# A decoder layer on one core: places of the shared TensorE units by a table, one projection row a slot earlier, residual rows fetched a slot ahead

## The reference

```
x = x + self_attention(layernorm(x))        # causal, q and k normalised per head, softmax
x = x + cross_attention(layernorm(x), ctx)  # per query row only the 32 largest of 512 scores enter the softmax
x = x + ffn(layernorm(x))                   # inner 2048, rows quantised to 8 bits, weights to -1, 0, 1
ffn(x) = quant(silu(quant(x) Wg) * (quant(x) Wu)) Wd
```

## Time and profile before

| | |
|---|---|
| median of 3 runs | 3952.01 us (3951.01 to 3952.15) |
| the profiled execution | 3955.8 us |
| its span, first to last instruction | 3954.0 us |
| mean granted TensorE clock | 0.86 of full speed |
| DVE busy / PE busy / ACT / POOL | 3219.5 / 3320.5 / 2451.1 / 1916.0 us |
| mean of one MAX8 (L876) / MATCH_REPLACE8 (L881) | 680 / 676 ns |
| chain that ended last | DVE 38%, PE 28%, POOL 13%, issue 9% |

### The profile page before, as it was taken

One profiled execution on the slowest core, in us unless ns is written; L12 is line 12 of the kernel. 1 busy time (PEld: TensorE's weight loads), 2 busy tenths in 40 slices (PEclk: granted clock), 3 DMA queues, 4 the chain that ended last, 5 costly groups with the idle time before them and its releaser, 6 DMA issues.

```text
span 3954.0 us, 61337 instructions
## 1 busy us (share of the span) xinstructions
PE 3320.5 (84%) x18502; PEld 2447.8 (62%) x18502; DVE 3219.5 (81%) x7571; ACT 2451.1 (62%) x4921; POOL 1916.0 (48%) x2444
## 2 busy tenths in 40 slices
PE   2587788998989989998989898998999898877765
PEld 1355576766666667666766676766766676555542
DVE  4311199999989999899989898899979998999961
ACT  3343466666766667666866676667766676555533
POOL 0123234446655465546654555445654564355435
PEclk7667888988989989988988898988898898887778
DMA  8112332332222222322222222322232221211100
GB/s 277 50 51 57 98 77 69 81 86 66 71 66 77 66 62 77 97 76 62 78 78 78 70 67 63 84 72 68 78 82 79 73 70 41 62 46 35 33 22 19
DMA packets 167443, 283.04 MB, mean 72 GB/s; under 512 B 40639, under 2 KB 52939, under 8 KB 166606
## 3 DMA queue, kind: packets, MB, share of 16 engines
q1 hardware_dynamic: 160782, 275.98, 25.6%
q10 hardware_dynamic: 6336, 3.15, 0.3%
HBM read 113.27 MB, written 31.46 MB: 37 GB/s over the span
## 4 chain that ended last, share of the span: by engine, by line
DVE 38%; PE 28%; POOL 13%; issue 9%; ACT 5%; SPq 3%; DMA 1%; DVEq 0%; POOLq 0%; ACTq 0%
DVE cW L881 17%; DVE top L876 14%; PE bank L682 6%; PE bank L607 5%; PE bank L654 4%; POOL srs L1147 3%; SPq L513 3%; PE bank L593 2%; POOL hh L1111 2%; DVE smx L1013 2%; PE bank L670 2%; PE bank L635 2%; POOL hh L1115 2%; PE bank L694 2%; PE bank L701 2%
## 5 line engine op out<-in xcount | busy, mean ns | idle before, releaser
L881 DVE MATCH_REPLACE8 cW<-top,cW 128x512 f32<-128x512 f32 x1536 | 1026.3, 676 | 0.0
L876 DVE MAX8 top<-cW 128x8 f32<-128x512 f32 x1536 | 980.8, 680 | 0.0
L797 ACT ACTIVATE PT<-bank 128x512 f32<-128x512 f32 (+3 forms) x1024 | 539.6, 527 | 363.5 <-PE bank L593 359.8
L1168 POOL TENSOR_TENSOR cS<-cS,cW 128x512 f32<-128x512 f32 x512 | 641.7, 1275 | 199.3 <-ACT cW L825 198.8
L607 PE MATMUL bank<-cv,PT 128*128 128x33 f32 x4096 | 589.0, 291 | 113.3 <-ACT PT L797 111.8
L607 PEld LDWEIGHTS bank<-cv,PT 128*128 128x128 f32 x4096 | 559.1, 211 | 148.1 <-ACT PT L797 141.6
L607 PEld LDWEIGHTS bank<-sv,PT 128*128 128x128 f32 x2560 | 404.8, 214 | 81.1 <-ACT PT L797 57.4
L1175 POOL TENSOR_SCALAR cnb<-top 128x2 f32<-128x2 f32 x256 | 49.0, 191 | 807.4 <-DVE top L876 793.1
L593 PE MATMUL bank<-ident,cS 128*128 128x128 f32 x2048 | 352.2, 300 | 82.4 <-POOL cS L1168 82.4
L825 ACT ACTIVATE cW<-cW,cnb 128x512 f32<-128x512 f32 x512 | 347.6, 733 | 118.5 <-DVE cW L881 118.1
L607 PE MATMUL bank<-sv,PT 128*128 128x33 f32 x2560 | 377.0, 282 | 37.2 <-ACT PT L797 36.0
(11 more groups left out here) (151 smaller groups left out, 6105.0 us busy)
## 6 DMA issues: line engine op xcount, KB each, us to landing
sk_stack<-part SPq DMA_DIRECT2D x512, 64.0 KB, 2.0
sq_stack<-part SPq DMA_DIRECT2D x512, 64.0 KB, 2.0
ck_stack<-part SPq DMA_DIRECT2D x512, 64.0 KB, 2.0
cq_stack<-part SPq DMA_DIRECT2D x512, 64.0 KB, 2.0
w_group<-wa_by_group SPq DMA_DIRECT2D x32, 768.0 KB, 4.5
w_group<-wc_by_group SPq DMA_DIRECT2D x32, 768.0 KB, 4.3
feed<-in_x SPq DMA_DIRECT2D x32, 256.0 KB, 3.0
feed<-in_ctx SPq DMA_DIRECT2D x32, 256.0 KB, 3.0
```

Of the source, the lines that this page charges most:

```text
L797: act.activation(PT[k][:, 0:n], turned_ps[k][:, 0:n], ACT.Copy).then_inc(turned_read, step("turned_read", label))
L876: dve.max(top8[:, j, r, :], src[:]).then_inc(topk, step("topk", (c, r, "max", j)))
L881: dve.match_replace(cW[j][:], top8[:, j, r, :], src[:], REPLACED).then_inc(topk, step("topk", (c, r, "replace", j)))
L1168: pool.tensor_tensor(cS[m % 2][j][:], cS[m % 2][j][:], cW[j][:], ALU.subtract).then_inc(cprob, step("cprob", (m, j)))
```

## The change

It puts the tables of `schedule(b)` in the place of the formulas, for each batch element b:

- cross tiles at slots 15, 17, 18, 19 (places 15, 1, 2, 3) for all but the last batch element.
- chunks, for b = 0 to 5: 4 early and late, 5 early and late, 6 late, 7 early, 8 early and late, 9 late, 10 early, 11 early, 13 early, 15 early, then in the next batch element 0 early and late, 1 early (as places). hT stands at places 6, 9, 14 and 3, and `down` at 7, 9, 14 and 5 (at 4 after b = 5). The first chunks of the next element follow at place 4. Element 6 has the old dense pattern, three slots later; element 7 is as before.
- `self_qkv` 0 goes from q = 0, cell 0, to the slot before (q = 3, cell 5); 1 and 2 go from cells 3 and 6 to 2 and 5; 3 goes from q = 1, cell 1, to cell 3. `self_out` goes to cell 4 where q = 2.
- DVE does `self_rows` one round later.
- SP issues weights and stack copies first in a slot, then the stores of the slot's own rows, and then fetches `x1res`, `x2res` and `xres` for the next slot.

```diff
+def schedule(b):
+    def dense(first):
+        chunks = [(first + 3 * t + r, early) for t in range(NT) for r in range(2) for early in (True, False)]
+        ends = tuple(first + 3 * t + 2 for t in range(NT))
+        return chunks, ends, ends
+    if b == NB - 1:
+        return ((15, 16, 17, 18), *dense(17))
+    if b == NB - 2:
+        return ((15, 17, 18, 19), *dense(20))
+    chunks = [(20, True), (20, False), (21, True), (21, False), (22, False), (23, True), (24, True), (24, False),
...
+    return (15, 17, 18, 19), chunks, (22, 25, 30, 35), (23, 25, 30, 36 if b == NB - 3 else 37)
...
 def cross_tile(s):
-    return tile_at(s, LAG + 15)
+    return next(iter(planned(s, 0, lambda at: at)), None)
 def x2_tile(s):
-    return tile_at(s, LAG + 16)
+    return cross_tile(s - 1)
...
-    g, q = self_group(s), s % NT
+    q = s % NT
+    g = s // NT + 2
+    if q == 3 and 0 <= g < NGROUPS:
+        u[5].append(("self_qkv", g, 0))
+    g = self_group(s)
-        for at, cell, unit in ((0, 0, ("self_qkv", g, 0)), (0, 3, ("self_qkv", g, 1)), (0, 6, ("self_qkv", g, 2)),
-                               (1, 1, ("self_qkv", g, 3)), (3, 2, ("self_kT", g)), (3, 3, ("self_qT", g))):
+        for at, cell, unit in ((0, 2, ("self_qkv", g, 1)), (0, 5, ("self_qkv", g, 2)),
+                               (1, 3, ("self_qkv", g, 3)), (3, 2, ("self_kT", g)), (3, 3, ("self_qT", g))):
...
-        u[3].append(("self_out", self_tile(s)))
+        u[4 if q == 2 else 3].append(("self_out", self_tile(s)))
...
@@ SP, in each slot @@
-                        t = x1_tile(s)
+                        t = self_tile(s)
                         if t is not None:
                             sp.wait_ge(x1_stats, upto("x1_stats", ("x1", t)))
                             sp.dma_start(rows(x1_rows, t), xres[:]).then_inc(x1_out, step("x1_out", t, 16))
-                        t = cross_tile(s)
+                        t = cross_tile(s + 1)
...
                             sp.dma_start(x1res[:], rows(x1_rows, t)).then_inc(x1res_in, step("x1res_in", t, 16))
-                        t = self_tile(s)
+                        t = self_tile(s + 1)
...
-                        for t in mlp_down(s):
+                        for t in mlp_down(s + 1):
...
@@ DVE, in each slot @@
+                        top(c, 1, ROUND_1)
                         self_rows(s)
-                        top(c, 1, ROUND_1)
@@ POOL @@
-                        for t, n in mlp_chunk(s, False):
+                        for t, n in mlp_chunk(s, True) + mlp_chunk(s, False):
```

More of the change, by code:

```diff
@@ L66, in x1_tile, with planned @@
     return tile_at(s, 15)
+def schedule(b):
[8 more added lines that the diff above has]
+    chunks = [(20, True), (20, False), (21, True), (21, False), (22, False), (23, True), (24, True), (24, False),
+              (25, False), (26, True), (27, True), (29, True), (31, True), (32, True), (32, False), (33, True)]
+    return (15, 17, 18, 19), chunks, (22, 25, 30, 35), (23, 25, 30, 36 if b == NB - 3 else 37)
+def planned(s, part, entry, tiles=NT):
+    out = []
+    for b in range(NB):
+        for i, at in enumerate(schedule(b)[part]):
+            if at == entry(s - LAG - SLOTS * b):
+                out.append(tiles * b + i)
+    return out
 def cross_tile(s):
-    return tile_at(s, LAG + 15)
+    return next(iter(planned(s, 0, lambda at: at)), None)
 def x2_tile(s):
-    return tile_at(s, LAG + 16)
+    return cross_tile(s - 1)
 def feeds(s):
@@ L99, in cross_group, with mlp_inner @@
     return g if 0 <= g < NGROUPS else None
[L102 to L106 removed]
 def mlp_chunk(s, early):
[L111 to L112 removed]
+    return [divmod(i, NF) for i in planned(s, 1, lambda at: (at, early), NT * NF)]
+def mlp_inner(s):
+    return planned(s, 2, lambda at: at)
 def mlp_down(s):
[L116 to L117 removed]
+    return planned(s, 3, lambda at: at)
 def cells(s):
     u = [[] for _ in range(CELLS)]
[L123 removed]
+    q = s % NT
[3 more added lines that the diff above has]
+    g = self_group(s)
     if g is not None:
[L125 to L126 removed]
+        for at, cell, unit in ((0, 2, ("self_qkv", g, 1)), (0, 5, ("self_qkv", g, 2)),
+                               (1, 3, ("self_qkv", g, 3)), (3, 2, ("self_kT", g)), (3, 3, ("self_qT", g))):
             if at == q:
@@ L140, in cells @@
         u[2].append(("self_oT", self_tile(s)))
-        u[3].append(("self_out", self_tile(s)))
+        u[4 if q == 2 else 3].append(("self_out", self_tile(s)))
     if x2_tile(s) is not None:
         u[4].append(("x2T", x2_tile(s)))
+    for t in mlp_inner(s):
+        for n in range(NF):
+            u[3 + n].append(("hT", t, n))
     for early, cell in ((True, 2), (False, 6)):
@@ L147, in cells @@
     for t in mlp_down(s):
-        for n in range(NF):
-            u[3 + n].append(("hT", t, n))
         u[7].append(("down", t))
@@ L437, in pipeline @@
                         C.plan("pool_rows", ("ln", t, k))
-                for t in mlp_down(s - 1):
-                    C.plan("h_dve", ("out", t))
                 for early, at in ((False, s - 1), (True, s)):
+                    for t in mlp_down(s - 1) if early else ():
+                        C.plan("h_dve", ("out", t))
                     for t, n in mlp_chunk(at, early):
@@ L556, in _ @@
                                 copy_part(unit, j)
+                        t = cross_tile(s)
+                        if t is not None:
+                            sp.wait_ge(dve_rows, upto("dve_rows", ("x2", t)))
+                            sp.dma_start(rows(x2_rows, t), x2t[:]).then_inc(x2_out, step("x2_out", t, 16))
+                        t = cross_tile(s + 1)
+                        if t is not None:
+                            if t:
+                                sp.wait_ge(dve_rows, upto("dve_rows", ("x2", t - 1)))
+                            sp.wait_ge(x1_out, upto("x1_out", t, 16))
+                            sp.dma_start(x1res[:], rows(x1_rows, t)).then_inc(x1res_in, step("x1res_in", t, 16))
+                        t = self_tile(s)
+                        if t is not None:
+                            sp.wait_ge(x1_stats, upto("x1_stats", ("x1", t)))
+                            sp.dma_start(rows(x1_rows, t), xres[:]).then_inc(x1_out, step("x1_out", t, 16))
                         for t in mlp_down(s - 1):
                             store_y(t)
+                        for t in mlp_down(s + 1):
+                            sp.wait_ge(x2_out, upto("x2_out", t, 16))
+                            if t:
+                                sp.wait_ge(y_out, upto("y_out", t - 1, 16))
+                            sp.dma_start(x2res[:], rows(x2_rows, t)).then_inc(x2res_in, step("x2res_in", t, 16))
+                        t = self_tile(s + 1)
+                        if t is not None:
+                            if t:
+                                sp.wait_ge(x1_out, upto("x1_out", t - 1, 16))
+                                sp.wait_ge(x1_norm, upto("x1_norm", (t - 1, 4)))
+                            sp.dma_start(xres[:], rows(x_rows, t)).then_inc(xres_in, step("xres_in", t, 16))
                     sp.wait_ge(x1_out, 16 * NTILES)
```

29 lines of the change are left out of this document (removed).

## The result

The changed kernel takes 3934.25 us (median of 7 runs, 3923.57 to 3938.94) beside 3952.15 us of the kernel before (median of 7 as well): ratio 0.9939, 95% interval 0.9924 to 0.9954. It is faster, by 0.6%, where I had forecast 3%: 3833 us, with a range from 3785 to 3925. The time lies outside the range.

What follows compares the result with a forecast made beforehand. DVE and PE were both busy over four fifths of the span, with 188 us of DVE waits in elements 1 to 5; terms there summed to -103, with elements 6 and 0 to -119, giving 3833 us, range 3785 to 3925.

Steps and rivals of the forecast that it cites:

- The weights: Cross weights load after the moved self_qkv 3, so PE stands at cross_v; +10 us, bounds 0 to +24, slack taking most.
- `x1res` a slot ahead: Row fetch issued up to a slot before use, so DVE's 22.3 us of waits for it go; -22, bounds -18 and -22.
- Late chunks: DVE's waits for the product in hh, mainly at places 3 and 11, shrink; -32 us, bounds -13 and -40.
- Probabilities: DVE's waits at place 3 for POOL's probabilities go, the early chunk being gone at place 2; -15 us, bounds 0 and -15.
- `self_out`: DVE's waits for PE's self_out at places 10 to 13 fall, place 10 giving at most about 4 of 8; -26 us.
- Reciprocal: DVE's waits before the reciprocal in norms, following PE's values of the slot before, fall; -15 us, bounds 0 and -20.
- `cross_out`: DVE's wait at place 15: the new down costs 3.6 us, a full-speed clock gives about as much back; -3, bounds +15 and -10.
- The waits move: Rival: PE stays late at place 10, waits reappear at places 7 and 15; -56 us, 3886, chance 0.25 for 3865 to 3935.
- PE becomes the bound: Rival: PE's mean clock falls below 0.81 as full places thin out; 4007 us at 0.79, chance 0.05 within slower's 0.09.
- The rule from the Trainium skill: Transposes do not count as activity for the clock gate, so places that lost projections could fall to half clock.
- The rival of no gain: Weights' stall reaches DVE whole (24 us), self_out and reciprocal waits stay; within 0.2% of 3952 us, chance 0.04.

Runs made afterwards that it cites:

- experiment 1: The changed kernel with self_qkv 3 moved back from cell 3 to cell 1 of its slot; 3856.04 us, ratio 0.9761 to the kernel before.
- experiment 2: The changed kernel, units in their new cells, with the cross weights' value columns in their own tile and load, issued a slot ahead; 3856.34 us, 0.9761.
- experiment 3: The changed kernel with the old places of cross tiles, chunks, hT and down; 4013.39 us, ratio 1.0154 to the kernel before.
- experiment 5: Experiment 1's kernel with SP's queue order as before the change, so without the prefetch; 3842.62 us, ratio 0.9723 to the kernel before.
- experiment 12: Experiment 8's kernel with SP's order as before the change; 3807.48 us, ratio 0.9633 to the kernel before.
- experiment 9: Experiment 1's kernel with the self group's weights loaded in the slot before, amid its stack copies; 3860.16 us, ratio 0.9764 to the kernel before.
- Experiment 8: Experiment 1's kernel with the early chunk of place 10 moved to place 11 and that of 11 to 12; 3817.56 us, 0.9658 to the kernel before.

## Why the prediction was wrong

**The weights (+10, bounds 0 to +24): the step that failed.** I had the mechanism and the places; the stall I had at 1.9 us at places 1 and 5 and about 1 at place 9, and in element 3 it measured 3.10, 2.46 and 1.57. Over elements 1 to 5 the stalls come to 34.4 us, more than the upper bound of 24 already. Experiments 1 and 2 put the price at 70 us and more. What failed is the sentence that PE's slack takes most of it, with the stall's full length as the upper bound. The slack itself was misread: 21.9 us a slot is PE's work as if at full clock, while the same rows have PE busy for 24.38 us a slot beside DVE's 24.55. Three things were left out of the bound. PE works at half clock behind the stall: `cross_v` took about 8.7 us at place 1, where each of its four tiles took 2.08 us with 1.16 at full speed. A late PE at the end of q = 1 is late in the slot behind it, and the delay is paid there where `cross_out` or `self_out` has DVE waiting (places 2 and 10, 4.5 and 4.7 us an element), and hardly at place 6 (0.4). And a slack that is a mean over slots does not help in the one slot whose reader waits; this last is argued from the places, not tested by itself.

**`x1res` a slot ahead (-22):** the wait went, by 14 us in the change and by all in experiment 1. But that it went was luck as far as the prefetch goes: experiment 3 has the prefetch and the wait, experiment 5 has neither and experiment 12 next to none. The table did it. SP's new order costs 10 to 13 us. Here another sentence failed, that SP's loop and row 0 a slot earlier cost nothing because the self group's load lands well before cell 5: at place 7 PE waits 5.80 us for it in experiment 1, and 3.56 with SP's old order. That this wait is the whole of the 10 to 13 us is not shown: experiment 9 took the wait away and won nothing, since place 10 lost what place 8 gained.

**Late chunks (-32)** came to -32.0, as forecast; place 6's late chunk costs little (0.8 us at place 7). **Probabilities (-15)** came to -7.8, half, and to -12.7 in experiment 1.

**`self_out` (-26):** in the change -1.7; with the load early -19.8. That POOL's chunk and `head_norm` in a row at q = 2 limit place 11 was right in kind: not DVE but PE waits there for the probabilities, 3.9 us, and `self_out` comes late to DVE behind it. Experiment 8 took this away, together with PE's chunk ahead of `self_out` at place 10, and won 38 us. I had it as a limit, and not as the next thing to take away.

**Reciprocal (-15)** came to +1.6, and to -12.2 with the load early.

**`cross_out` (-3):** +22.5, and +12.8 with the load early. Of the +22.5, 16 us are at place 2, behind the stall of place 1, where the prediction had none. At place 15 the wait is 2.9 us an element in the change, 4.2 in experiment 1 and 1.8 in experiment 2, all with the `down` at place 14, and 2.5 before; so the `down` does not decide it alone, and what does is open. The upper bound (+15) would have held without the load.

**The rivals.** "The waits move" was the right kind, and its -56 for elements 1 to 5 is nearer to the measured -29 than the forecast; the measured time is inside its bracket of 3865 to 3935 by less than a microsecond. It named place 10, place 15 and the weights, and these at 15 us. "PE becomes the bound" did not come true as a fall of the mean clock, which rose from 0.90 to 0.92 and stood at 0.94 in experiment 1. The rule from the Trainium skill (TensorE: Matmul & The Clock Gate, Part 4: PE-mode transpose) beside it forecast a fall at places with hT in place of projections; place 14 of element 3, with its hT and `down`, ran at 1.00 in the change, and so did place 9 with four hT in experiment 1. Most of the low clocks looked at come behind waits of PE (3.10 us at place 1, 4.22 at place 9 in experiment 9), but not all: place 4 of the change has 0.94 on average, and in element 3 the clock falls there, at 1826.9, behind the hT of place 3 and turned probabilities, where PE's longest wait since 1812 was 0.41 us. That would fit the rule, but the same units ran at 1.00 there in experiment 1; what this fall comes from is open. The rival of no gain had the weights reach DVE whole, and put 24 us on it, again without the half clock.

With row 3 in cell 1 the kernel would have been inside the range. The sum for elements 1 to 5 would have been -113 without the weights' term; experiment 1 has -87. Element 6, forecast at -14, has -9.9 there and +5.4 in the change. The head, forecast at 0, gave 15.3 us in the change's profile, which the prediction had no term for.

## What to carry to other kernels

When a unit moves, follow what waits for its end, not only its own place: here a weight load hung on a projection row, and the row two cells later cost 70 us with no more work on any engine. A stall on an engine near its bound is charged with the half clock behind it and at the next slot that has a reader, not against a mean slack; and if one table entry stacks two long jobs on a slower engine (POOL's chunk ahead of `head_norm`), moving it may be worth a lot (38 us here, a part of it by PE's own lighter load). A prefetch takes its place in the queue from something else: before it goes in, look at what stands behind it and when that is needed. Here it took away no wait and cost 10 to 13 us.

## What the runs showed of the hardware

Being late can be faster. In experiment 1 PE came to its first hT of place 9 at 1924.85, found its input ready, and ran the place at a granted clock of 1.00. In experiment 9 it was there 4.4 us earlier, at 1920.46, waited 4.22 us, and ran the place at 0.71. At the first hT the two are level; the third came 5.3 us later in experiment 9, since the work between was done at half clock, and place 10 took 36.3 us instead of 30.8. The same holds at `cross_v`: a wait of 3.10 us was followed by four tiles at 2.08 us instead of 1.16, so that the stall cost as much again behind it (3.7 us) as in it.
